# Gate products of fourteen sequences as three products of a rounded part and a rest, with another order of the roundings on ScalarE

## What is computed

```python
x_conv = causal_depthwise_conv(xn, conv_w) + conv_b      # four taps
r_t = sigmoid(x_conv @ W_r.T + b_r)
i_t = sigmoid(x_conv @ W_i.T + b_i)
a_t = sigmoid(log_a) ** (8 * r_t)
h_t = a_t * h_(t-1) + sqrt(1 - a_t * a_t) * i_t * x_conv
s   = rmsnorm(h @ W_out.T) * gamma
```

```python
x = x + local_attention(shift(x)) @ wo
h = layernorm(shift(x)) @ w1 + b1
x = x + (a * gelu(g)) @ w2 + b2        # a, g are the halves of h
```

## Time and profile before

| | |
|---|---|
| median of three runs | 1276.41 us |
| the profiled execution | 1274.72 us |
| its span (first to last instruction) | 1272.9 us |
| TensorE busy | 1235.6 us (97%) |
| ScalarE busy | 1146.8 us (90%) |
| GpSimd busy | 1113.6 us (87%) |
| VectorE busy | 1079.3 us (85%) |
| granted TensorE clock, mean | 0.999 of full speed |

### The profile page before, as it was taken

The page is one execution under the profiler, slowest core; times in us unless marked ns, Lnnn a source line. Parts: engine busy times, 40 slices in busy tenths (PEclk is TensorE's granted clock), DMA queues, the critical chain, the costliest instruction groups (busy, mean ns, idle before and its releaser), DMA issues.

```text
span 1272.9 us, 39536 instructions
## 1 busy us (share of the span) xinstructions
PE 1235.6 (97%) x14442; PEld 1004.6 (79%) x14443; DVE 1079.3 (85%) x1921; ACT 1146.8 (90%) x3651; POOL 1113.6 (87%) x780
## 2 busy tenths in 40 slices
PE   7999999999999999999989999999999999999997
PEld 4788888888888887666767888888888888887776
DVE  7898888888888886788889999999999999984777
ACT  5899999999999999777779999999999999998886
POOL 4889999999999998479779999999999999984775
PEclk9999999999999999999999999999999999999999
DMA  5123222322233231020011222222222222211323
GB/s 172 49 62 81 72 72 77 83 74 72 73 79 79 64 81 44 26 63 1 1 30 39 48 60 60 62 57 56 57 55 56 56 60 62 50 44 35 91 76 91
DMA packets 64129, 78.59 MB, mean 62 GB/s; under 512 B 7872, under 2 KB 38144, under 8 KB 63936
## 3 DMA queue, kind: packets, MB, share of 16 engines
q1 hardware_dynamic: 63936, 76.06, 23.3%
HBM read 21.72 MB, written 4.26 MB: 20 GB/s over the span
## 4 chain that ended last, share of the span: by engine, by line
PE 84%; POOL 5%; ACT 5%; DVE 3%; issue 3%; DMA 0%; ACTq 0%; SPq 0%; DVEq 0%; POOLq 0%
PE ps L223 66%; PE ps L273 9%; PE ps L283 4%; PE ps L286 4%; POOL t L1363 2%; ACT P L720 2%; POOL hxr L1363 1%; POOL P L1363 1%; DVE t L1060 1%; PE ps L228 0%; ACT sqk L696 0%; PE ps L483 0%; DVE side L1200 0%; ACT PT L712 0%; POOL hT L1363 0%
## 5 line engine op out<-in xcount | busy, mean ns | idle before, releaser
L720 ACT ACTIVATE P<-ps,nm 128x128 f32<-128x128 f32 x1024 | 344.4, 418 | 0.0
L223 PE MATMUL ps<-wqkv,hT 128*128 128x512 f32 x1152 | 314.5, 410 | 7.3 <-DVE t L1060 5.4
L1363 POOL TENSOR_TENSOR t<-t 128x1024 f32<-128x1024 f32 x128 | 305.9, 2390 | 15.2 <-DVE t L1060 10.7
L1363 POOL TENSOR_TENSOR P<-P,rden 128x512 f32<-128x512 f32 x256 | 289.6, 1141 | 25.2 <-DVE rden L1097 21.8
L1363 POOL TENSOR_TENSOR t<-t,rr 128x1024 f32<-128x1024 f32 x128 | 243.9, 1905 | 22.9 <-ACT rr L705 21.8
L223 PEld LDWEIGHTS ps<-wqkv,hT 128*128 128x128 f32 x1152 | 201.5, 189 | 69.4 <-issue 22.3
L720 ACT ACTIVATION_READ_ACCUMULATOR P<-ps,nm 128x1 f32 x1024 | 236.1, 231 | 0.0
L1071 DVE TENSOR_TENSOR t<-ps,tabl 128x512 f32<-128x512 f32 x256 | 164.1, 682 | 38.9 <-ACT sqk L696 36.2
L1363 POOL TENSOR_TENSOR hxr<-hxf,hxr 128x512 fp32r<-128x512 f32 (+1 forms) x93 | 127.4, 1398 | 69.6 <-ACT hxr L778 69.4
L1090 DVE TENSOR_REDUCE nm<-ps 128x4 f32<-128x512 f32 x256 | 173.4, 679 | 5.7 <-PE ps L223 5.6
L712 ACT ACTIVATE PT<-ps 128x1024 f32<-128x1024 f32 x128 | 129.7, 1013 | 30.6 <-PE ps L273 30.5
(11 more groups left out here) (150 smaller groups left out, 2564.9 us busy)
## 6 DMA issues: line engine op xcount, KB each, us to landing
Vs<-Vn SPq DMA_DIRECT2D x224, 128.0 KB, 2.3
B<-rows SPq DMA_DIRECT2D x32, 256.0 KB, 3.2
side<-in_x SPq DMA_DIRECT2D x17, 256.0 KB, 3.2
A<-X SPq DMA_DIRECT2D x16, 256.0 KB, 2.5
norm<-X SPq DMA_DIRECT2D x32, 128.0 KB, 2.2
norm<-X SPq DMA_DIRECT2D x32, 127.8 KB, 2.3
hsh<-X SPq DMA_DIRECT2D x31, 128.0 KB, 2.3
hsh<-X SPq DMA_DIRECT2D x31, 127.8 KB, 2.3
```

The lines of the kernel that those rows point to most:

```text
L223: return e.matmul(o, lhsT, rhs, start=start, stop=stop, skip_group_check=True)
L720: k = act(P[:, g, :], ps[:, 3 + s, (g % 4) * 128:(g % 4 + 1) * 128], ACT.Exp, bias=nm[:, g:g + 1], accum_out=den(s)[:, g % 4:g % 4 + 1])
L1363: return e.tensor_tensor(o, a, b_, op)
```

## The change

Sequences 1 to 14 get split gate products. ScalarE copies the convolution's output into `cvr[0]` (fp32r), GpSimd writes the rest into `cvr[1]`, and W_r and W_i are split once into `wrr`, so that a gate product is three fp32r products. Sequences 0 and 15 stay as they were. In layer 0 ScalarE now does `split_hx(b, 0)` and `split_hx(b, 1)` in turn b, right after the first tap of `conv(b+1)`, and not at the head of turn b + 1. The two table loads of turn 2 move ahead of `gelu(2, 2)`, in both layers. The new tiles lie in space that was only kept free.

```diff
-            sp_("kept", [128, 2048 - L])
+            wrr = sp_("wrr", [128, 2, 2, 128], F32R)
+            cvr = sp_("cvr", [128, 2, L], F32R)
...
TensorE
+            def gate_product(b, g):
+                if not 0 < b < NB - 1:
+                    return mm(ps[:, 7, :], wr[:, g, :], cv[b % 2])
+                for j, (p, q) in enumerate(THREE):
+                    k = mm(ps[:, 7, :], wrr[:, q, g, :], cvr[:, p, :], j == 0, j == 2)
+                return k
+
             def gates(b):
-                e.wait_ge(s_cv, 3 * (b + 1))
+                if 0 < b < NB - 1:
+                    e.wait_ge(s_cvlo, b)
+                else:
+                    e.wait_ge(s_cv, 3 * (b + 1))
+                if b == 1:
+                    e.wait_ge(s_wrlo, 1)
...
-                mm(ps[:, 7, :], wr[:, 0, :], cv[b % 2]).then_inc(s_gr, 1)
+                gate_product(b, 0).then_inc(s_gr, 1)
             def gates2(b):
                 e.wait_ge(s_r, b + 1)
-                mm(ps[:, 7, :], wr[:, 1, :], cv[b % 2]).then_inc(s_gi, 1)
+                gate_product(b, 1).then_inc(s_gi, 1)
...
ScalarE
+            def round_wr():
+                e.wait_ge(s_tpk, NT)
+                act(wrr[:, 0, :, :], wr[:, 0:2, :], ACT.Copy).then_inc(s_wrhi, 1)
+
+            def round_cv(b):
+                e.wait_ge(s_gi, b)
+                e.wait_ge(s_cv, 3 * (b + 1))
+                act(cvr[:, 0, :], cv[b % 2], ACT.Copy).then_inc(s_cvhi, 1)
...
-                    if 0 < b < NB:
+                    if l and 0 < b < NB:
                         split_hx(l, b - 1, 0)
                         split_hx(l, b - 1, 1)
                     if b < NB:
                         gelu(l, b, 0)
                     if 0 < b < NB:
                         split_hx(l, b - 1, 2)
+                    if l == 0 and 0 < b < NB - 1:
+                        round_cv(b)
                     if b < NB:
                         gelu(l, b, 1)
...
+                    if b == 2:
+                        e.preload_act_table_set(ATTN)
+                        log_var(l, NB - 1)
+                        root_var(l, NB - 1)
+                        e.preload_act_table_set(MIXED)
                     if b < NB:
                         gelu(l, b, 2)
...
                         gates(b)
                         if b + 1 < NB:
                             conv(b + 1)
+                            split_hx(l, b, 0)
+                            split_hx(l, b, 1)
...
                         gates2(b)
+                        if b == 0:
+                            round_wr()
...
-                    if b == 2:
-                        e.preload_act_table_set(ATTN)
-                        log_var(l, NB - 1)
-                        root_var(l, NB - 1)
-                        e.preload_act_table_set(MIXED)
...
VectorE
                     if n == NT:
                         e.wait_ge(s_hxf, 3 * NB)
+                        e.wait_ge(s_gi, NB - 1)
...
+            def rest_wr():
+                e.wait_ge(s_wrhi, 1)
+                e.tensor_tensor(wrr[:, 1, :, :], wr[:, 0:2, :], wrr[:, 0, :, :].bitcast(F32), ALU.subtract).then_inc(s_wrlo, 1)
...
                     if l == 0 and b < NB - 1:
                         gates2(b)
+                    if l == 0 and b == 0:
+                        rest_wr()
...
GpSimd
+            def rest_cv(b):
+                e.wait_ge(s_cvhi, b)
+                tt(cvr[:, 1, :], cv[b % 2], cvr[:, 0, :].bitcast(F32), ALU.subtract).then_inc(s_cvlo, 1)
...
                     if 0 <= b - 1 < (NB - 1 if l else NB):
                         for j in range(3):
                             split_hx(l, b - 1, j)
+                    if l == 0 and 0 < b < NB - 1:
+                        rest_cv(b)
                     if b + 1 < NB:
                         split_hn(l, b + 1)
```

More of the change, by code:

```diff
@@ L205, in program @@
                                "s_hnhi", "s_gl", "s_r", "s_ti", "s_w2hi", "s_hxhi", "s_cv0", "s_h0hi"))
-        s_dec, s_rt0, s_rt, s_osq, s_rms0, s_rms, s_s, s_th = (
-            sem(n_) for n_ in ("s_dec", "s_rt0", "s_rt", "s_osq", "s_rms0", "s_rms", "s_s", "s_th"))
+        s_dec, s_rt0, s_rt, s_osq, s_rms0, s_rms, s_s, s_th, s_wrhi, s_cvhi = (
+            sem(n_) for n_ in ("s_dec", "s_rt0", "s_rt", "s_osq", "s_rms0", "s_rms", "s_s", "s_th", "s_wrhi", "s_cvhi"))
         s_cst, s_tabm, s_t2, s_ss0, s_ss, s_nm, s_rd, s_kt, s_wlo, s_w2lo, s_h0, s_hxlo1 = (
@@ L213, in program @@
         s_hn = [sem("s_hn0"), sem("s_hn1")]
[L214 to L218, removed]
+        s_hxf, s_xf, s_cv, s_xi, s_a2n, s_hs, s_osum, s_eg, s_em, s_eo, s_wrlo = (
+            sem(n_) for n_ in ("s_hxf", "s_xf", "s_cv", "s_xi", "s_a2n", "s_hs", "s_osum", "s_eg", "s_em", "s_eo", "s_wrlo"))
+        s_zero, s_nmr, s_nrm, s_add, s_tn, s_pn, s_hi, s_h, s_hnlo, s_a2, s_in, s_hxlo, s_wlo1, s_tabm1, s_pm, s_po, s_cvlo = (
+            sem(n_) for n_ in ("s_zero", "s_nmr", "s_nrm", "s_add", "s_tn", "s_pn", "s_hi", "s_h", "s_hnlo", "s_a2", "s_in", "s_hxlo", "s_wlo1", "s_tabm1", "s_pm", "s_po", "s_cvlo"))
         def tensor(e):
```

## The result

The changed kernel took 1312.9 us (median of four runs, 1312.37 to 1316.81) beside 1276.32 us for the kernel before: a ratio of 1.0288 (95% interval 1.0264 to 1.0312), 36.6 us slower. The forecast was 19.1 us slower, with a range that ended at 1303. The profiled execution took 1313.11 us with a span of 1311.3, so its parts can be set against the 1274.72 and 1272.9 of before.

A forecast was written before the change was run, and what follows sets the result against it. TensorE bounds the kernel now; a 9.4 us loop through GpSimd would replace its 7.99 us turn. Loops +12.9, start +2.4, turns 1 and 2 +1.1 and +1.5, turn 9 +1.0, end +0.5, layer 1 -0.3: +19.1, 1295.5 us; range 1278 to 1303.

The forecast's parts named there:

- The closed loop: Layer 0 feed-forward: each gate product waits, through ScalarE and GpSimd's `rest_cv`, on the one before; 9.4 us against 7.99.
- The fixed part: The loop without GpSimd's instructions: three gate products, tanh, first convolution tap, rounding and hand-overs; 2.96 us.
- GpSimd's four: Three `hxr` subtractions and one `cvr` on GpSimd within the loop; 5.08 to 6.6 us, taken as 6.45.
- Turns 1 and 2: Layer norm sums and table loads delay the early turns: `gates(2)` +1.1 us at 10.5, table loads +1.5 us.
- Turn 9: GpSimd's two extra pieces for `hT`, 2.67 us, do not fit between `rest_cv` and the next `hxr`: +1.0 us.
- Turn 3 of layer 1: With the table loads moved ahead, the roundings behind them come earlier: -0.3 us (-1.8 to +0.5).
- The signs: Expected in the trace: blocks 9.4 us apart, TensorE idle 1.5 to 1.8 us before `gates`, taps about 4 us.
- all three taps and then `gates2` meet GpSimd's four: VectorE's taps and `gates2` run beside GpSimd's chain, slowing both; GpSimd's four put near the upper end, 6.45 us.
- 0.5 us of cover: ScalarE's `round_cv` ends near 7.3 us, GpSimd is free for `rest_cv` at about 7.8, so the rounding costs nothing.
- The fourth rival: Each meeting costs GpSimd a whole VectorE instruction, and `round_cv` comes late: +20 us more, 1315 us; chance 0.06.
- the start: `gates(1)` follows the `conv(1)` tap, rounding and GpSimd's four, at 525.9 instead of 523.45: +2.4 us.
- under 0.5 us each and hidden in turns 0 and 1: The weights' rounding and rest, done once each on 256 columns, add nothing to the time.

The follow-up runs named there:

- the two kernels with extra products: Changed kernel plus eight unused TensorE products ahead of `gates`: in all 14 turns, 1312.34 us; only in turns 1, 4, 6, 9, 11 and 13, 1316.99 us.

## Why the prediction was right and wrong

**Right:**
- *The closed loop.* The mechanism is the one named, and without `rest_cv` the loss is gone. The fixed part was 2.96 us in the forecast and is 3.03 (2.98 and 0.05); GpSimd's four were 6.45 and are 5.99; the loop was 9.4 and is 9.02, wherever `gates2` does not interfere. With `gates2` in PSUM the whole kernel is 19.3 us slower than before, beside 19.1 in the forecast. The nearness is partly luck: from `gates(1)` to `gates(14)` that kernel takes 123.2 us where the forecast had 125.8, and its `gates(1)` is 3.1 us later than forecast, so that two errors cancel.
- *Turns 1 and 2.* With `gates2` in PSUM from sequence 2 on, `gates(3)` comes 10.9 us after `gates(2)`, as forecast (9.4 + 1.5), though by a loop that is 0.4 shorter and an extra that is 0.4 longer. `gates(2)` comes 12.5 after `gates(1)`, not 10.5; that is the clock, see below. Turn 9 adds 0.5 us and not 1.0. Turn 3 of layer 1 takes 8.30 us (1212.49 to 1220.79), 0.26 less than in the earlier trace rows; the forecast was 0.3.
- *The signs.* The chain on GpSimd (`hxr` x3, `cvr`, `hnr`), its start about 3 us after the gate product, and taps of 4.16 us all show. TensorE's idle time ahead of each `gates` is 1.1 us, not 1.5 to 1.8, by the shorter loop.

**Wrong, by 17 us: the price of a meeting on VectorE.** The step that failed is "all three taps and then `gates2` meet GpSimd's four. Only the first meeting is partial", with its price from the earlier trace rows, about half an instruction each, so that `round_cv` "costs nothing while 0.5 us of cover lasts". That price is about right for the taps: two of the three take 1.66 us instead of 0.75 alone, 4.16 together. It is wrong for `gates2`: issued during the third `hxr` it lets two to four further GpSimd instructions go first and takes 3.6 to 5.4 us. The earlier trace rows do not show that: the `gates2` at 592.27 is issued during the second `hxr` and comes in before the third. Even behind the third the kernel before has one that comes in, ahead of an `hnr` that follows without a gap (553.27, 1.74 us):

```profile
552.76 1.10 DVE L1204 SCALAR_TENSOR_TENSOR A<-oT 128x512 f32<-128x512 f32 x1
```

The 0.5 us of cover were gone at once: ScalarE's first tap waits for `gates2`, the other taps for VectorE, and `round_cv` waits 21.1 us for the last tap. Putting one input of `gates2` in PSUM takes this cost away: 1.0288 to 1.0151 is 17.5 us, and to 1.0160 with the variant from sequence 0 on. From `gates(1)` to `gates(14)` the two traces differ by 142.0 - 123.2 = 18.8 us. This takes in what the long waits cost through the clock.

The fourth rival, 1315 us with 0.06, came nearest in time and named `round_cv` as what would be late. Its price was also of another kind, one whole VectorE instruction lost by GpSimd. GpSimd's third `hxr` loses no more than before; it is VectorE that loses, and by several GpSimd instructions. The Trainium skill (SBUF — State Buffer, Who interferes with whom) has the two engines exclude each other for the whole instruction. The trace agrees that they don't overlap, but the instruction that waits does not come next: in the first timeline above four GpSimd instructions go ahead of it.

**Mis-sized: the start.** `gates(1)` comes 5.5 us later relative to turn 1, forecast +2.4. GpSimd is done for it 6.7 us after the turn's start, near the 7.0 of the forecast; TensorE then waits for `rest_wr`. The step "under 0.5 us each and hidden in turns 0 and 1" counted the duration of `rest_wr` (0.41 us, right) and not the place on VectorE, where whatever stands there is held.

**Left out: the order's own price.** The forecast took the earlier roundings as part of the loop only. Alone they cost 13 us, 5 with `gates2` in PSUM. In the changed kernel it is not a separate term, as the old order costs the same there for another reason.

**Counted by nobody: the clock.** Six stretches at 1.2 GHz make the mean clock of the stage 0.90. It is not the main loss, since the two kernels with extra products were no faster as a whole, but it is not nothing: the stage was 3.6 and 2.7 us shorter in them. It also explains `gates(2)`. The forecast had 5.31 us from `gates(1)` to `up(2)`. In the kernel with PSUM from sequence 2 on this takes 7.67 us at a mean clock of 0.63, with `down` at 4.04 us instead of 2.26, and in the one with the rest on VectorE as well 5.09 at 1.00 (525.24 to 530.33).

The account of the 38.4 us of the profiled executions, from the start of turn 1: 5.5 for `gates(1)`, 142.0 - 109.3 = 32.7 for the 13 loops, 1.1 behind them, and -0.9 since turn 1 itself began earlier. Of the 32.7, 123.2 - 109.3 = 13.9 are the loop as it is without the long `gates2` of the later turns, and 18.8 are those, with the half clock behind the waits that they make.

**What stays open.** Which GpSimd instructions a waiting VectorE instruction lets go first. In the changed kernel a tap that is issued during one `hxr` comes in before the next, each time; a `gates2` issued during the third does not come in before `cvr`, `hnr`, and what follows them. But in the kernel before a `gates2` came in ahead of `hnr`, and in the kernel with the order alone, and in the one without the rest, single taps also stayed out past a second `hxr` (3.54 and 4.87 us). No rule covers all of these, and no run tried to separate the GpSimd instructions from each other. How much of the 18.8 us is the clock is known only for the five loops named above. It also stays open why the kernel without the rest is 12 us faster than the order alone; the two differ in the gate products and in what `gates` waits for. A version that has the split and is faster than before was not found.

## What to carry to other kernels

A moved instruction is to be priced together with what stands behind it on the other engine: where VectorE with two SBUF inputs meets a chain of GpSimd instructions without a gap, take the whole chain as the upper bound of its length (here 5.4 us for 0.67), and ask who waits for it. An operand that has a PSUM bank to stay in removes the meeting, at the price of holding the bank. And before work is saved on the engine that is the bound, look whether the saving puts another engine into a loop with it: 0.3 us of TensorE a turn were bought here with a loop 1 us longer than the turn.

## What the runs showed of the hardware

- VectorE's `gates2` takes 0.67 us alone or with a PSUM input, 1.1 to 2.4 beside one to three GpSimd instructions, and 3.4 to 5.5 where it is issued during the third `hxr` of a chain and two to four more come first. `rest_wr` takes 0.41 us, and 5.16 in that place.
- A VectorE tap and a GpSimd `hxr` that meet in a row of such meetings take 1.65 to 1.68 and 1.72 to 1.75 us in the loops of 9.02 us, with 0.75 and 1.26 alone.
- After TensorE's six waits of 3.3 to 5.3 us in the changed kernel its granted clock was 0.50 for a while. `gates` of three products then took up to 1.65 us where it takes 0.96 at the full clock, and the nine of `down` 2.9 to 4.0 instead of 2.26. Five loops took 53.35 us at a mean clock of 0.87, and 49.59 at 1.00.
- A place earlier by one gelu for two table loads with their Ln and Exp gave a ratio of 0.9969, of which the trace shows 2.3 us where they stand.
